# Reordering the feed-forward stage of a recurrent-attention and feed-forward kernel

## What is computed

```python
xn = layernorm(x)
def ffn(x):                                   # 4096 tokens, D = 512, FF = 1408
    routed = sigmoid(x @ w_router + b_router) > 0.5
    h = x + (rmsnorm(x, norm1_w) @ wv + bv) @ wo
    h2 = rmsnorm(h, norm2_w)
    mlp = (silu(h2 @ w_gate) * (h2 @ w_up)) @ w_down
    return where(routed, h + mlp, x)
# of the attention, computed beside it in the same stage for every token and head:
beta = sigmoid(b);  g = -exp(A_log) * softplus(a + dt_bias)      # [b, a] = xn @ w_ba.T
out = x + attention(xn, ...) * silu(ffn(xn))
```

## Time and profile before

| | |
|---|---|
| median of 3 runs | 4370.98 us (4370.25 to 4373.52) |
| the profiled execution | 4373.52 us, with a span of 4371.1 us from first to last instruction |
| feed-forward stage | 0 to 1094 us |
| busy share of the span | PE 98%, DVE 65%, ACT 56%, POOL 34% |
| mean granted TensorE clock | 0.994 of full speed |

### The profile page before, as it was taken

How to read it: one execution, slowest core, us unless ns; L and a number is a source line. 1 busy time by engine, 2 the same in 40 slices (tenths; PEclk the granted TensorE clock), 3 DMA queues, 4 the chain that set the end, 5 groups by cost and what they waited for, 6 DMA issues and landing times.

```text
span 4371.1 us, 86611 instructions
## 1 busy us (share of the span) xinstructions
PE 4291.9 (98%) x32312; PEld 3276.9 (75%) x32312; DVE 2823.6 (65%) x6326; ACT 2462.7 (56%) x6253; POOL 1497.6 (34%) x1686
## 2 busy tenths in 40 slices
PE   7999999999899999999999999999999999999998
PEld 5778778777677777777777777777777777777776
DVE  4555555554566666776777666676777777766674
ACT  1222222222566667666766666666666766666675
POOL 2222222222133333333333333344443334433344
PEclk8999999999999999999999999999999999999999
DMA  4100000002100000000000011011111111111111
GB/s 133 35 20 29 31 21 27 31 21 86 38 18 21 21 21 28 24 21 21 23 23 21 23 47 55 21 55 43 38 43 35 38 38 35 38 45 35 35 36 42
DMA packets 115521, 154.71 MB, mean 35 GB/s; under 512 B 32416, under 2 KB 59040, under 8 KB 115104
## 3 DMA queue, kind: packets, MB, share of 16 engines
q1 hardware_dynamic: 79008, 93.94, 6.5%
q10 hardware_dynamic: 36096, 55.24, 4.0%
HBM read 113.73 MB, written 35.42 MB: 34 GB/s over the span
## 4 chain that ended last, share of the span: by engine, by line
PE 70%; DVE 1%; ACT 1%; POOL 1%; issue 1%; POOLq 0%; ACTq 0%; DVEq 0%
PE bank L1057 21%; PE bank L1354 10%; PE bank L1061 10%; PE bank L1631 10%; PE bank L1539 3%; PE bank L1525 2%; PE bank L1565 2%; PE bank L1500 2%; PE bank L1477 2%; PE bank L1253 1%; PE bank L1190 1%; PE bank L1254 1%; PE bank L1616 1%; PE bank L1106 1%; PE bank L1147 1%
## 5 line engine op out<-in xcount | busy, mean ns | idle before, releaser
L1057 PE MATMUL bank<-xtile,wt 128*128 128x259 f32 x4096 | 1095.0, 394 | 21.9 <-DVE vraw L1087 16.2
L1057 PEld LDWEIGHTS bank<-xtile,wt 128*128 128x128 f32 x4096 | 722.3, 191 | 143.8 <-DVE vraw L1087 45.5
L1411 ACT ACTIVATE xyinv<-bank 128x512 f16<-128x512 f32 x768 | 453.5, 593 | 275.3 <-PE bank L1354 272.7
L1631 PE MATMUL bank<-wot,xnt 128*128 128x512 f32 x1024 | 542.3, 619 | 0.8 <-ACT xnt L1624 0.8
L1061 PE MATMUL bank<-wt,xtile 128*128 128x512 f32 x1024 | 523.9, 615 | 0.0
L1387 DVE TENSOR_TENSOR wlev<-bank,mask 128x256 f16<-128x256 f32 x768 | 316.7, 418 | 293.5 <-PE bank L1354 288.7
L1320 POOL TENSOR_TENSOR ltl<-ltm,lth 128x512 f16<-128x512 f32 x128 | 149.5, 1168 | 764.3 <-ACT lth L1314 764.3
L1087 DVE SCALAR_TENSOR_TENSOR vraw<-bank,taps,vraw 128x256 f32<-128x256 f32 x768 | 368.5, 480 | 62.3 <-ACT vraw L1080 44.3
L439 PE MATMUL bank<-hb,wt 128*128 128x128 f32 x2816 | 375.2, 277 | 11.8 <-POOL hb L409 6.4
L439 PEld LDWEIGHTS bank<-hb,wt 128*128 128x128 f32 x2816 | 349.0, 193 | 34.3 <-issue 21.5
L1306 POOL TENSOR_TENSOR ltm<-ltm,mask 128x512 f32<-128x512 f32 x128 | 159.3, 1244 | 604.4 <-DVE ltm L1294 604.4
(11 more groups left out here) (192 smaller groups left out, 9146.9 us busy)
## 6 DMA issues: line engine op xcount, KB each, us to landing
grows<-row_scratch ACTq DMA_DIRECT2D x126, 256.0 KB, 3.2
xtile<-xt_scratch ACTq DMA_DIRECT2D x30, 518.0 KB, 3.8
xn<-x SPq DMA_DIRECT2D x32, 256.0 KB, 3.9
xt_scratch<-xt SPq DMA_DIRECT2D x16, 512.0 KB, 4.2
g_scratch<-sel SPq DMA_DIRECT2D x32, 256.0 KB, 2.0
part_scratch<-prow SPq DMA_DIRECT2D x32, 256.0 KB, 2.0
prow<-part_scratch SPq DMA_DIRECT2D x32, 256.0 KB, 2.6
sel<-g_scratch SPq DMA_DIRECT2D x32, 256.0 KB, 2.9
```

The source lines that it names most:

```text
L1057: j = pe.matmul(b_p[:, 0:WIN], wt[:, k, c:c + P], xtile[:, par, k, :], **st)
L1411: act.activation(dst, b_inv[p][:].rearrange("p (a h b s) -> p a h b s", a=2, h=HEADS, s=z), ACT.Copy).then_inc(s[f"xy_sb{p}"], 1)
L1631: i = pe.matmul(b_o[:], xnt[:, h], wot[:, h], start=(h == 0), stop=(h == GV - 1))
```

## The change

The three pieces of combined weights become two, of 6 and 5 column tiles; the second stands ahead of gate 3 (`FIRST // 2`). The list `first` goes away, so that the first round of products follows the same `front` as all others. In `front`, `soft` 1, `soft` 2, `soft` 3 and `cum` of unit u now stand among the gates of unit u-1, `keep` j is done at once behind `dve_back` j, every step of the front stands one gate earlier than before, and the step `rates` is part of `cum`. For unit 0 the whole front, and with it the opening of unit 1, stands ahead of the first combined weights. The opening of unit u+1 is interleaved with `down` as stats, down 0, normalise, down 1, router. SP stores the gates of unit u where it stored those of unit u-1. In `attention` two semaphores are added to count the steps of `pool_rms`; the waits and their meaning stay as they were. The feed-forward stage loses two semaphores.

```diff
-        KH, PIECES = KT // 2, (0, 3, 7, FT)
+        KH, FIRST = KT // 2, 6 * P
...
-        def dve_combine(dve, piece):
+        def dve_combine(dve, half):
-            f = slice(PIECES[piece] * P, PIECES[piece + 1] * P)
-            dve.wait_ge(s[f"g_in{piece}"], 32)
+            f = slice(0, FIRST) if half == 0 else slice(FIRST, FF)
+            dve.wait_ge(s["g_in"], 32 * (half + 1))
...
-            if u == 0 and f in PIECES:
-                pe.wait_ge(s["comb"], 4 * PIECES.index(f) + 4)
+            if u == 0 and f * P in (0, FIRST):
+                pe.wait_ge(s["comb"], 4 if f == 0 else 8)
...
-        front = ["gate", "gate", ("cum",), "gate", ("rates",), ("columns", 0), "gate", ("columns", 1), "gate", ("attn", 0), "gate", ("scale", 0), ("ba",), ("attn", 1), "gate",
-                 ("scale", 1), ("soft", 0), "gate", ("back", 0), "gate", ("back", 1), ("tokens",), "gate", "gate"]
-        first = ["gate", "gate", ("combine", 1), "gate", ("stats",), ("normalise",), ("soft", 1), "gate", ("router",), "gate", ("soft", 2), ("combine", 2), "gate", ("soft", 3), "gate",
-                 ("cum",), ("columns", 0), "gate", ("rates",), ("columns", 1), ("attn", 0), "gate", ("scale", 0), ("ba",), ("attn", 1), "gate", ("scale", 1), ("soft", 0), "gate",
-                 ("back", 0), ("back", 1), ("tokens",)]
+        front = ["gate", "gate", ("columns", 0), "gate", ("columns", 1), "gate", ("attn", 0), "gate", ("scale", 0), ("ba",), ("attn", 1), "gate", ("scale", 1), ("soft", 0),
+                 "gate", ("back", 0), ("soft", 1), "gate", ("soft", 2), ("back", 1), ("tokens",), "gate", ("soft", 3), "gate", "gate", ("cum",)]
+        opening = [("stats",), ("normalise",), ("router",)]
+        order = [(step, 0) for step in opening]
+        for u in range(UNITS_F + 1):
             f = 0
+            for step in front:
+                if step != "gate" and u < UNITS_F:
+                    order.append((step, u))
+                elif step == "gate" and u:
+                    if u == 1 and f * P == FIRST // 2:
+                        order.append((("combine", 1), 0))
                     order.append((("gate", f), u - 1))
                     if f:
                         order.append((("rest", f - 1), u - 1))
                     f += 1
-            order.append((("rest", FT - 1), u - 1))
-            if u == 1:
-                order += [(("keep", j), 0) for j in range(NJ)]
-            if u < UNITS_F:
-                order += [(("soft", part), u) for part in (1, 2, 3)] + [(("keep", j), u) for j in range(NJ)]
-            if u + 1 < UNITS_F:
-                order.append((("stats",), u + 1))
-            order.append((("down", 0), u - 1))
-            if u + 1 < UNITS_F:
-                order += [(("normalise",), u + 1), (("router",), u + 1)]
-            order.append((("down", 1), u - 1))
+            if u:
+                order.append((("rest", FT - 1), u - 1))
+            order += merged([(("down", j), u - 1) for j in range(NJ)] if u else [], [(step, u + 1) for step in opening] if u + 1 < UNITS_F else [])
+            if u == 0:
+                order.append((("combine", 0), 0))
...
-                for piece in range(3):
-                    f = slice(PIECES[piece] * P, PIECES[piece + 1] * P)
-                    sp.dma_start(wg_sb[:, :, f], kp(w_gate)[:, :, f]).then_inc(s[f"g_in{piece}"], 16)
-                    sp.dma_start(wu_sb[:, :, f], kp(w_up)[:, :, f]).then_inc(s[f"g_in{piece}"], 16)
+                for f in (slice(0, FIRST), slice(FIRST, FF)):
+                    sp.dma_start(wg_sb[:, :, f], kp(w_gate)[:, :, f]).then_inc(s["g_in"], 16)
+                    sp.dma_start(wu_sb[:, :, f], kp(w_up)[:, :, f]).then_inc(s["g_in"], 16)
...
                     elif kind == "back":
                         dve_back(dve, u, *i)
-                    elif kind == "keep":
                         dve_keep(dve, u, *i)
```

More of the change, by code:

```diff
@@ L196, in feed_forward @@
         N_SOFT, SOFT_STEPS = SERIES + 11, (3, 5, SERIES - 2, 5)
-        names = ["c_in", "r_in", *(f"w_in{e}" for e in range(KT)), "g_in0", "g_in1", "g_in2", "d_in", "set", "z_out", "bvb", "wvo_ps", "wvo_sb", "cb_ps", "cb_sb",
+        names = ["c_in", "r_in", *(f"w_in{e}" for e in range(KT)), "g_in", "d_in", "set", "z_out", "bvb", "wvo_ps", "wvo_sb", "cb_ps", "cb_sb",
                  "x_in0", "x_in1", "stat", "mvs", "rst", "xnd", "sqd", "scr", "r1a", "r1d", "kpt", "xc",
@@ L430, in dve_combine @@
             dve.tensor_tensor(s3[:, :, f], a11[:, :, f], a21[:, :, f], ALU.subtract).then_inc(s["comb"], 1)
-            dve.wait_ge(s["comb"], 4 * piece + 2)
+            dve.wait_ge(s["comb"], 4 * half + 2)
             dve.tensor_tensor(s2[:, :, f], s1[:, :, f], a11[:, :, f], ALU.subtract).then_inc(s["comb"], 1)
-            dve.wait_ge(s["comb"], 4 * piece + 3)
+            dve.wait_ge(s["comb"], 4 * half + 3)
             dve.tensor_tensor(s4[:, :, f], a12[:, :, f], s2[:, :, f], ALU.subtract).then_inc(s["comb"], 1)
@@ L617, in dve_cum @@
             dve.tensor_scalar(past, past, -1.0, None, ALU.mult).then_inc(s["gset"], 1)
-        front = ["gate", "gate", ("cum",), "gate", ("rates",), ("columns", 0), "gate", ("columns", 1), "gate", ("attn", 0), "gate", ("scale", 0), ("ba",), ("attn", 1), "gate",
-                 ("scale", 1), ("soft", 0), "gate", ("back", 0), "gate", ("back", 1), ("tokens",), "gate", "gate"]
-        first = ["gate", "gate", ("combine", 1), "gate", ("stats",), ("normalise",), ("soft", 1), "gate", ("router",), "gate", ("soft", 2), ("combine", 2), "gate", ("soft", 3), "gate",
-                 ("cum",), ("columns", 0), "gate", ("rates",), ("columns", 1), ("attn", 0), "gate", ("scale", 0), ("ba",), ("attn", 1), "gate", ("scale", 1), ("soft", 0), "gate",
-                 ("back", 0), ("back", 1), ("tokens",)]
-        assert front.count("gate") == FT and first.count("gate") == FT
-        order = [((kind, *i), 0) for kind, *i in [("stats",), ("normalise",), ("router",)] + [step for step in front if step != "gate" and step[0] not in ("cum", "rates")] + [("combine", 0)]]
-        for u in range(1, UNITS_F + 1):
-            f = 0
-            for step in first if u == 1 else front:
-                if step == "gate":
+        front = ["gate", "gate", ("columns", 0), "gate", ("columns", 1), "gate", ("attn", 0), "gate", ("scale", 0), ("ba",), ("attn", 1), "gate", ("scale", 1), ("soft", 0),
+                 "gate", ("back", 0), ("soft", 1), "gate", ("soft", 2), ("back", 1), ("tokens",), "gate", ("soft", 3), "gate", "gate", ("cum",)]
+        assert front.count("gate") == FT
+        opening = [("stats",), ("normalise",), ("router",)]
+        order = [(step, 0) for step in opening]
+        for u in range(UNITS_F + 1):
+            f = 0
+            for step in front:
[4 more added lines that the diff above has]
+                        order.append((("combine", 1), 0))
                     order.append((("gate", f), u - 1))
@@ L681, in _ @@
                 sp.wait_ge(s["x_in1"], 16)
-                for piece in range(3):
-                    f = slice(PIECES[piece] * P, PIECES[piece + 1] * P)
-                    sp.dma_start(wg_sb[:, :, f], kp(w_gate)[:, :, f]).then_inc(s[f"g_in{piece}"], 16)
-                    sp.dma_start(wu_sb[:, :, f], kp(w_up)[:, :, f]).then_inc(s[f"g_in{piece}"], 16)
-                    if piece == 0:
+                for f in (slice(0, FIRST), slice(FIRST, FF)):
+                    sp.dma_start(wg_sb[:, :, f], kp(w_gate)[:, :, f]).then_inc(s["g_in"], 16)
+                    sp.dma_start(wu_sb[:, :, f], kp(w_up)[:, :, f]).then_inc(s["g_in"], 16)
+                    if f.start == 0:
                         load(1)
-                for piece in range(3):
-                    sp.wait_ge(s[f"g_in{piece}"], 32)
+                sp.wait_ge(s["g_in"], 64)
                 sp.dma_start(wd_sb[:], kp(w_down)).then_inc(s["d_in"], 16)
@@ L692, in _ @@
                 load_small(sp, r, conv_w)
+                gates_out(0)
                 sp.wait_ge(s["set"], 2)
@@ L701, in _ @@
                         load(u + 1)
-                    gates_out(u - 1)
+                    if u < UNITS_F:
+                        gates_out(u)
                     if u == UNITS_F:
@@ L757, in _ @@
                         dve_soft(dve, u, *i)
-                    elif kind == "rates":
+                    elif kind == "cum":
                         dve_cum(dve, u)
@@ L949, in attention @@
             "eh_sb", "el_sb",
[L950 removed]
+            "ks_ps", "qs_ps", "r_sb", "t_sb", "e_ps", "e_sb", "su_ps", "s_sb", "o_ps", "o_sb", "xf_sb", "sn_sb", "rm1_sb", "rm_sb", "xn_sb",
             "xt_ps", "xt_sb",
@@ L1592, in act_squares @@
             if n:
-                act.wait_ge(s["xn_sb"], 3 * n - 2)
+                act.wait_ge(s["rm1_sb"], n)
                 act.wait_ge(s["sn_sb"], n)
@@ L1601, in pool_rms @@
             if n:
[L1602 to L1606, removed]
+                pool.wait_ge(s["xn_sb"], n)
```

(6 more changed lines are left out.)

4 lines of the change are left out of this document (removed).

## The result

The changed kernel takes 4402.68 us (median of 4 runs, 4402.53 to 4403.26), the kernel before 4371.55 us on the same chips: +31.1 us, a ratio of 1.0072 with a 95% interval of 1.0053 to 1.0089. The forecast was 4411.5, 4384 to 4436, slower: the sign and the range held, and the forecast +40.5 was 9.4 us too high (11.1 by the spans of the two profiled executions). The span grew from 4371.1 to 4400.5 us. PE's busy time hardly moved (4291.9 us in the earlier trace rows); the page of the changed kernel says

What follows compares the result with a forecast made beforehand. PE, busy 98% of the span, was taken as the bound, so only its waits count. Start +6.0 and later units +34.5 gave +40.5 us on the median 4371: 4411.5, range 4384 to 4436.

Steps and rivals of the forecast that it cites:

- Later units, 15 x 2.3 = 34.5 us: In 15 rounds with an interleaved front, PE waits 2.1 us ahead of gate 10 and 0.2 us at `rest` 10.
- the share of DVE's own work, 0.7: Ahead of gate 10: DVE's 9.2 us chain ends the sums of gate 8 at 17.1, due at 16.5; PE waits 0.7 us.
- the 1.3 us of POOL: DVE's loss beside POOL before the sums of gate 8: about 0.5 in `keep` 0, 0.4 in `soft` 2, 0.4 in `keep` 1.
- the 0.2 at `rest` 10: Allowance of 0.2 us a unit for `soft` 3 meeting `tokens` and a `hid`, which could delay the outs of gate 8.
- the port loss: DVE held up by POOL at shared ports in later units; the rival without it: wait 0.7 us, 4387.5 us, chance 0.16.
- The backlog: Rival: in later units each `soft` 3 operation waits for POOL, `rest` 10 about 2 us more; 4.3 a unit, 4441.5, chance 0.13.
- Covered costs: Later units: late `cum` hidden with 2.7 us to spare before `down` needs the last `hid`; router behind `down` 1 with 0.3.
- Start of gate 0, 65.2 us: First round: DVE's extra work ahead of the first combined piece makes PE start gate 0 at 65.2, 19.2 us later.
- The prediction's last part: Signs to look for, among them: PE's waits for L587, for ACT's copy and for L434 at 60 us are gone.
- Gate 3 waits 1.0 + 7.4 - 0.4 = 8.0 us: First round: PE waits 8.0 us ahead of gate 3 while DVE makes the second combined piece of five tiles.
- the 4.4 us of slow running: First round: of 8.2 us lost to PE's lower clock and filling up after waits, 4.4 remain, with two idle spells.
- the forecast +6.0: Net of the start: gate 0 19.2 us later, first round 12.3 shorter, `cum` of unit 0 done ahead 0.9 less.

Runs made afterwards that it cites:

- e6: Changed kernel with POOL's `hid` and `tokens` cut to one column of each block of 128, other engines' instructions the same; 4380.02 us.
- e8: Changed kernel with `keep` 1 alone moved behind `rest` 10, under `down`; 4389.95 us.
- e5: Changed kernel with normalise and router again ahead of `down` 1; 4403.17 us.
- e2: Changed kernel with PE waiting for the second combined piece ahead of gate 3 instead of gate 6; 4413.21 us.
- e4: Changed kernel with both keeps moved behind `rest` 10, under `down`; `soft` 1 to 3 and `cum` stay among the gates; 4367.79 us.
- e7: Kernel before with another first round alone: combined pieces 0 and 1 made ahead of the first sums, later steps reordered; 4361.90 us.

## Why the prediction was right, and where it was not

- **Later units, 15 x 2.3 = 34.5 us: right, in sum and in its parts.** Measured 15 x 2.32 = 34.8. Gate 10 was forecast at 18.6 us from zero and came at 18.46; the share of DVE's own work, 0.7, is e6's 0.68 to 0.75; the 1.3 us of POOL are the 0.5, 0.4 and 0.35 us in the rows after; the 0.2 at `rest` 10 is 0.21. One of these parts needed luck: the prediction called `keep` 0 beside `hid` a tie and put its 0.5 us in the sum without a reason why DVE should lose it. DVE lost it in every round; had it won, the same layout would give about 15 x 0.5 = 7.5 us less.
- **The rivals of those units fell.** Without the port loss the time would have been 4387.5: e6 builds that case, with 4380.0; the 4387.5 has the error of the start in it. The backlog (4.3 us a unit) did not come: two of the five operations of `soft` 3 met a POOL operation (0.64 and 0.68 us), not all. In e8 a milder form of it appeared.
- **Covered costs: right.** The router behind `down` 1 costs nothing (e5), the late `cum` does not delay `down` (the last `hid` ends at 455.2, 29.7 us from zero, forecast about 30), the attention stage kept its length within 1 us.
- **Start of gate 0, 65.2 us: right** (65.05), with two errors of 0.5 us that cancel. The first piece took 65.05 - 57.89 = 7.2 us, not 7.7, since POOL lengthened none of its four operations (1.75 or 1.76 us each); from the end of `soft` 3 (47.77) through `cum` to the opening (51.14) it took 3.4 us, not 2.9. The prediction's last part says that the wait for L587 is gone; it is not, but stands at 47.83 now, inside that stretch.
- **"Gate 3 waits 1.0 + 7.4 - 0.4 = 8.0 us": wrong, and it is the whole error.** The first piece has six tiles, so PE needs the second at gate 6. DVE makes it ahead of gate 3 to have it ready, and the wait in `pe_gate` stands at `FIRST`, not at `FIRST // 2`. I took the place where DVE makes the piece for the place where PE waits for it. The wait was 0. With it went 2.3 of the 4.4 us of slow running. The first round took 50.02 - 2.3 = 47.7 us without the wait of the later units, forecast 58.0: 10.3 us, which is the difference between the forecast +6.0 and the measured -4.4. With 10.4 us here, -0.3 in the later units and 1.0 in the attention stage the forecast is 11.1 us too high by the spans; by the medians, which scatter by a us or two, it is 9.4. e2 builds the assumed wait in and gets the forecast time.

## What to carry to other kernels

Lay the work of the engine that is late out against the due times of the engine that is the bound, one step after another with the waits in between: its average load (DVE 65%) says nothing about them. Removing 3.3 us of work brought the whole wait of 2.3 us in e4, and removing 1.55 us brought only 0.75 in e8, because other waits came up. A step whose result is not needed for a long time (here POOL's `tokens`) still has a price if it reads SBUF beside an engine that is near its due time. For each semaphore in a diff, read the place of the wait and the place of the work apart from each other.

## What the runs showed of the hardware

- What DVE loses beside POOL does not shrink with the size of its own operation: L421, 512 columns, loses 0.34 us (1.09 against 0.75), and L580, 64 columns, takes 0.19 us alone and 0.63 to 0.73 us in all 16 instances of the changed kernel beside POOL. POOL is slowed in the same way, 0.89 and 1.05 instead of 0.73 us beside `keep`.
- The granted clock stayed at 1.00 through the rounds with a PE wait of 1.8 us, and in the kernel before for the 7.6 us behind the wait of 3.17 us (60.28 in the earlier trace rows). It was 0.60 for 7.7 us behind one of 3.61 us (e7) and 0.80 for 7.5 us behind one of 7.86 us (e2), but 0.50 for 6.9 us behind one of 7.38 us in the kernel before (83.15 in the earlier trace rows). So the length of the wait alone does not say how much slow running follows it. As an estimate from these figures, the wait of 3.6 us in e7 cost 3.6 + 0.40 x 7.7 = 6.7 us.
